# Projections phase of a two-block vision kernel: key and value turns and their sums in one stretch of small tiles, relu of the queries on ScalarE, the next image loaded in four pieces

## The chip, the core and the metric

The kernel runs on one core of one Trainium2 chip. The metric is the device time of one execution in microseconds (us); shorter is better. The engines are TensorE (PE in the rows; PEld is its weight load), VectorE (DVE), ScalarE (ACT), GpSimd (POOL) and SyncE (SP), each with its own queue of instructions, ordered among each other by semaphores only.

## The reference, cut to what matters

For 8 images of 256 channels and 64x64 pixels the reference does a window mixing with a residual, and then, on the group-normed result, a linear attention with a residual:

```python
qkv = einsum('bchw,oc->bohw', gn(x), w_qkv)          # 256 -> 768 channels
y = depthwise 5x5 of qkv, then grouped 1x1            # "convolved heads"
mqkv = concat([qkv, y], axis=1)                       # 64 heads of 3*8 channels
q, k = relu(first 8), relu(second 8);  v = third 8, and a row of ones
vk = einsum('bhdn,bhen->bhde', v, k)                  # sums over the 4096 pixels
out = einsum('bhde,bhen->bhdn', vk, q);  out = out[:8] / (out[8] + eps)
x = x + batchnorm(w_proj @ out)
```

The projections phase, which the change is about, computes `qkv` for the unconvolved heads, stores it (for the convolution) and the relu of q (for the output phase), and forms `vk` of these heads: keys and values are turned, so that pixels lie on the partitions, and multiplied.

## The kernel before

Four phases follow each other: window mixing, projections, convolved heads, output. All is written out by hand; each engine's order is the order of the code, and every wait is a semaphore count.

**Projections.** 8 images, and for each 8 chunks of 512 pixels (`NCH = 8`), 64 chunks in all. Images 0, 1 and the last two are written out; the four between run in a hardware loop over pairs (`over_image_pairs`). For each chunk:

- ScalarE makes the normalised pixels of the chunk ahead (`normal`, two halves, L975), and their high part (`high`, L986); VectorE subtracts for the low part (`split`, L1217).
- TensorE forms six output tiles, `product(b, n, 0..5)` (L1125), each of 6 matmuls of 512 columns, in three PSUM banks: tile j uses bank j % 3, and must wait until the tile that had it is copied out. Order: key 0, value 0, key 1, value 1, query 0, query 1.
- ScalarE copies the keys (`key(u)`, L1045) and query 0; VectorE copies the values (`value(n, u)`, L1270) and query 1 (L1305).
- TensorE turns tile pair u (`turn`, L1139: 8 transposes of 128x128) after products 2 and 4, ScalarE takes them out of PSUM (`turned(u)`, L1050 with relu for the keys and L1053), and after product 5 TensorE adds this chunk's share to the sums (`sum_vk`, L1151: 16 matmuls of 32 columns of weights for each pair).
- VectorE and GpSimd write differences and borders of every tile into `stage` (`keys_values`, `queries`; DVE L1223 to L1229, POOL L902 to L937), which SyncE's queue stores to `qkv_scratch`; GpSimd makes the relu of the queries (L941), and SyncE stores it to `qr_scratch`. `stage` has two buffers, used in turn by even and odd chunks: a buffer is written again when its stores have landed.
- In chunks 1 to 4 VectorE also takes the statistics of the next image (`moments`, `norm_moments`, one quarter a chunk), after the copy of query 1; at the end of chunk 4 it gathers them, in chunk 5 `centre` and in chunk 5 `variance` follow, with two small matmuls of TensorE between (`means`, `variances`), in chunk 6 `scale`.
- At the end of an image ScalarE issues the load of the image after the next, 4 MB in one transfer (L1087); its statistics are taken from chunk 1 of the next image on.

Of the kernel before, what the change touches and what calls it, by code (L numbers as in the profile page):

```python
# [25 lines left out]
ALU = mybir.AluOpType  # L26
ACT = mybir.ActivationFunctionType
# [153 lines left out]
def make_constants(nc, ctx, two_phases, K):  # L181
# [7 lines left out]
    K["vk"] = sb("vk_table", [P, KT, B, D + 1])  # L189
# [14 lines left out]
    K["p_mv"] = sb("pmv", [P, CT, 2])  # L204
    K["p_norm"] = norm_tiles(sb, lambda name: ctx.enter_context(nc.semaphore(name)), "p")
# [45 lines left out]
def window_mixing(nc, K, x_in, w_mix, b_mix, w_qkv, w_dw, x1_dram, taps_dram):  # L251
# [3 lines left out]
    with ExitStack() as ctx:  # L255
# [30 lines left out]
        def norm_of(b):  # L286

            return (0, K["p_norm"][0], K["p_mv"], K["p_norm"][1], None) if b == B else (b, T, mv, ns, mean)
# [448 lines left out]
def projections(nc, K, x1_dram, qkv_dram, qr_dram, w_pw, bn_in, taps_dram, sorted_dram):  # L737
# [3 lines left out]
    with ExitStack() as ctx:  # L741
# [25 lines left out]
        vT = sb("vT", [P, 2, 4, NSQ, VS])  # L767
# [8 lines left out]
        t_ps = psum("pt_ps", [P, 2, 512])  # L776
        vk_ps = psum("vk_ps", [P, 2, 512])
        stat_bank = psum("pstat_ps", [P, 512])
        stat_ps = stat_bank[:, 0:4]
        pw_ready, pw_turned = K["pw_ready"], sem("pw_turned")  # L780
        std_in, std_out, bn_link = sem("bn_var"), sem("bn_std"), sem("bn_chain")
        qs_ready_late = sem("qs_ready_late")

        w_loaded, w_turned, w_split = K["wq_loaded"], sem("wq_turned"), sem("wq_split")
        zeroed, bordered = sem("zeroed"), sem("bordered")
        x_loaded = [sem(f"x1_loaded{i}") for i in range(2)]
# [8 lines left out]
        vk_full, vk_taken = sem("vk_full"), sem("vk_taken")  # L795
# [23 lines left out]
        def _(sp):  # L819
# [17 lines left out]
            def body(i, last):  # L837
                for par in range(2):
# [14 lines left out]
                    def queries(n):  # L853
# [4 lines left out]
                        if last and par == 1 and n == NCH - 1:  # L858
                            sp.wait_ge(qs_ready_late, 1)
                        else:  # L860
                            own.wait_ge(qs_ready, NCH * b + n + 1)
# [4 lines left out]
                    for n in range(NCH):  # L866
                        keys_values(n, 0)
                        if n > 0:
                            queries(n - 1)
                        keys_values(n, 1)  # L870
# [9 lines left out]
        def cells_free(eng, g):  # L880

            at_least(eng, t_full, 4 * (g - 1))
            at_least(eng, kv_diff, 2 * (g - 1))
            at_least(eng, kv_odd, 2 * (g - 1))
# [7 lines left out]
        def _(pool):  # L892
            pool.memset(vT[:, :, :, :, SQ:VS], 1.0).then_inc(zeroed, 1)

            def body(i, last_body):
                for par in range(2):
# [7 lines left out]
                    def border(n):  # L904
# [5 lines left out]
                        pool.memset(stage[:, n % 2, :, :, :, row, :].rearrange("p t a k x -> p (t a) k x"), 0.0)\  # L910
                            .then_inc(bordered, 1)
# [17 lines left out]
                    def queries(n, end=False):  # L929
# [4 lines left out]
                        at_least(pool, K["qr_stored"][n % 2], 32 * (4 * b + n // 2))  # L934
# [3 lines left out]
                        if end:  # L938
                            return
                        for t in range(2):  # L940
                            last = pool.tensor_scalar(qs[:, n % 2, t, :], qw[:, n % 2, t, :], 0.0, None, ALU.max)  # L941
                        last.then_inc(qs_ready, 1)

                    for n in range(NCH):
                        if n % 4 < 2:
                            border(n)
                        keys_values(n, 0)
                        if n > 0:
                            queries(n - 1)
                        keys_values(n, 1)  # L950
                    queries(NCH - 1, last_body and par == 1)
# [3 lines left out]
        def _(act):  # L955
# [58 lines left out]

            def pointwise(step):
# [5 lines left out]
                elif step == 1:  # L1021
                    act.wait_ge(pw_turned, 1)
                    act.activation(K["pw"][:, 0:4 * HT, :].rearrange("p g o -> p (g o)"), stat_bank[:, :], ACT.Copy)\
                        .then_inc(pw_ready, 1)
                elif step == 2:
# [3 lines left out]
                    act.activation(K["pw"][:, 4 * HT:6 * HT, :].rearrange("p g o -> p (g o)"), stat_bank[:, 0:2 * P], ACT.Copy)\  # L1029
                        .then_inc(pw_ready, 1)  # L1030

            def body(i, last_body):
                for par in range(2):
                    b = 2 * i + par
                    for n in range(NCH):
# [4 lines left out]

                        def key(u):
# [5 lines left out]
                        def turned(u):  # L1047
                            act.wait_ge(t_full, 4 * g + 2 * u + 1)
                            at_least(act, vk_full, g)
                            act.activation(kT[:, u, :, :].rearrange("p a c -> p (a c)"), t_ps[:, 0, :], ACT.Relu)\  # L1050
# [1173 lines left out]
```

## Time and profile before

| | us |
|---|---|
| median of 3 runs | 2488.25 |
| lowest, highest | 2484.59, 2489.66 |
| profiled execution: time, span | 2490.49, 2488.8 |
| busy in the span: TensorE, VectorE, ScalarE, GpSimd | 2364.8, 1992.4, 1495.8, 1099.0 |

The profiled execution is one further run; its span is the time from the first to the last instruction. Busy shares are means over four phases with different limits, so the projections are read by themselves. In the rows a start is in us from the span's start, and the projections lie from about 261 to 1015 us. Matmuls overlap, so the busy time of TensorE says little: what counts is the distance from one start to the next.

### The profile page before, as it was taken

How to read it: one execution, taken by the hardware profiler on the slowest of the kernel's cores; microseconds unless marked ns; L12 is line 12 of the kernel's file. 1: busy time of each engine (PE TensorE's matmuls, PEld its weight loads, DVE VectorE, ACT ScalarE, POOL GpSimd, SP SyncE). 2: the span in 40 equal slices, each digit the busy share in tenths (PEclk: the TensorE clock that was granted, in tenths of full speed). 3: DMA queues.
4: the chain of work that ended last, by engine and by line, in shares of the span. 5: the costliest groups of instructions: out<-in, count | busy, mean ns of one | idle time of the engine just before them, and what ended most of it. 6: DMA issues, size and time to landing. Idle time of an engine off the chain costs nothing. (4 is left out here: it accounts for less than half of the span.)

```text
span 2488.8 us, 66780 instructions
## 1 busy us (share of the span) xinstructions
PE 2364.8 (95%) x25485; PEld 1886.2 (76%) x25485; DVE 1992.4 (80%) x2652; ACT 1495.8 (60%) x1864; POOL 1099.0 (44%) x1477
## 2 busy tenths in 40 slices
PE   5999799999999999799999999999999889999998
PEld 5889687777787788577888888888888656666666
DVE  7887588787688786788888888888888578888775
ACT  5777576665566566566677677667767433443342
POOL 6722387787787787300000000000000068888887
PEclk9999899999999999899999999999999999999999
DMA  7874688988889889988888888888888677777774
GB/s 283 342 293 177 212 301 313 325 294 306 307 281 323 320 282 321 267 204 204 206 213 208 208 208 210 207 207 212 210 206 209 215 251 271 279 278 271 270 271 135
DMA packets 300877, 628.38 MB, mean 252 GB/s; under 512 B 50688, under 2 KB 252160, under 8 KB 291456
## 3 DMA queue, kind: packets, MB, share of 16 engines
q1 hardware_dynamic: 295616, 590.90, 77.1%
q10 hardware_dynamic: 4048, 31.11, 3.5%
q0 software_dynamic: 1008, 3.67, 0.4%
q8 instruction: 125, 2.05, 0.3%
q14 instruction: 80, 0.66, 0.1%
HBM read 327.81 MB, written 300.94 MB: 253 GB/s over the span
## 5 line engine op out<-in xcount | busy, mean ns | idle before, releaser
L1901 POOL TENSOR_TENSOR ql<-image,qh 128x1024 fp32r<-128x1024 f32 x128 | 305.3, 2410 | 971.4 <-ACT qh L1929 971.4
L1555 PE MATMUL c_ps<-dh,wh 128*128 128x512 f32 x1152 | 463.5, 402 | 17.5 <-DVE wl L1706 13.1
L1470 ACT ACTIVATE dh<-image 128x1632 fp32r<-128x1632 f32 x192 | 301.5, 1570 | 266.7 <-PE c_ps L1555 250.6
L1555 PE MATMUL c_ps<-dh,wl 128*128 128x512 f32 x1152 | 455.0, 395 | 0.0
L1555 PE MATMUL c_ps<-dl,wh 128*128 128x512 f32 x1152 | 453.6, 394 | 1.3 <-issue 1.3
L1664 DVE TENSOR_TENSOR dl<-image,dh 128x1632 fp32r<-128x1632 f32 x192 | 356.4, 1856 | 72.2 <-ACT dh L1470 72.2
L1125 PE MATMUL o_ps<-xh,wqh 128*128 128x512 f32 x768 | 320.8, 418 | 11.0 <-issue 7.6
L1125 PE MATMUL o_ps<-xl,wqh 128*128 128x512 f32 x768 | 304.6, 397 | 0.0
L1125 PE MATMUL o_ps<-xh,wql 128*128 128x512 f32 x768 | 303.4, 395 | 0.0
L1555 PEld LDWEIGHTS c_ps<-dh,wh 128*128 128x128 f32 x1152 | 217.7, 189 | 70.1 <-DVE wl L1706 13.2
L1555 PEld LDWEIGHTS c_ps<-dl,wh 128*128 128x128 f32 x1152 | 217.3, 189 | 53.4 <-issue 1.3
L1555 PEld LDWEIGHTS c_ps<-dh,wl 128*128 128x128 f32 x1152 | 217.5, 189 | 45.8
L941 POOL TENSOR_SCALAR qs<-qw 128x512 f32<-128x512 f32 x126 | 234.2, 1874 | 0.0
L1045 ACT ACTIVATE kv<-o_ps 128x512 f32<-128x512 f32 x128 | 76.9, 601 | 260.2 <-PE o_ps L1125 256.7
L2037 PE MATMUL z_ps<-qh,fh 128*128 128x512 f32 x512 | 208.5, 407 | 5.2 <-ACT qh L1929 3.6
L1950 ACT ACTIVATE zs<-z_ps,bn_shift 128x512 f32<-128x512 f32 x64 | 44.0, 687 | 281.6 <-PE z_ps L2037 281.6
L2037 PE MATMUL z_ps<-qh,fl 128*128 128x512 f32 x512 | 200.7, 392 | 0.0
L2037 PE MATMUL z_ps<-ql,fh 128*128 128x512 f32 x512 | 200.5, 392 | 0.0
L1270 DVE COPY kv<-o_ps 128x512 f32<-128x512 f32 x128 | 87.9, 687 | 123.8 <-PE o_ps L1125 123.1
L975 ACT ACTIVATE xn<-image,p_nb,p_sc 128x512 f32<-128x512 f32 (+2 forms) x160 | 175.8, 1121 | 8.4 <-PEq L255 8.4
L902 POOL TENSOR_TENSOR ptick<-ident 128x1 f32<-128x1 f32 x224 | 95.4, 426 | 184.7 <-DMA qkv_scratch<-stage 78.5
L1125 PEld LDWEIGHTS o_ps<-xh,wqh 128*128 128x128 f32 x768 | 146.4, 191 | 39.7 <-issue 14.1
(210 smaller groups left out, 5024.0 us busy)
## 6 DMA issues: line engine op xcount, KB each, us to landing
qkv_scratch<-stage SPq DMA_DIRECT2D x384, 408.0 KB, 4.0
image<-qkv_scratch SPq DMA_DIRECT2D x189, 816.0 KB, 6.3
qr_scratch<-qs SPq DMA_DIRECT2D x128, 256.0 KB, 3.0
yq_scratch<-qy SPq DMA_DIRECT2D x64, 512.0 KB, 6.7
image<-qr_scratch SPq DMA_DIRECT2D x128, 256.0 KB, 6.2
image<-yq_scratch SPq DMA_DIRECT2D x128, 256.0 KB, 5.9
ox<-x_scratch SPq DMA_DIRECT2D x8, 4096.0 KB, 14.8
out<-ox SPq DMA_DIRECT2D x7, 4096.0 KB, 12.7
```

Source lines behind the costliest of these rows:

```text
L902: pool.tensor_tensor(tick[:, k:k + 1], K["ident"][:, 0:1], K["ident"][:, 1:2], ALU.add)
L941: last = pool.tensor_scalar(qs[:, n % 2, t, :], qw[:, n % 2, t, :], 0.0, None, ALU.max)
L975: last = act.activation(dst[:, :, to:to + rows, :], src[:, :, of:of + rows, :], ACT.Identity, bias=T["nb"][:, ct:ct + 1], scale=T["sc"][:, ...
L1045: act.activation(kv[:, n % 2, 2 * u, :], o_ps[:, (2 * u) % 3, :], ACT.Copy).then_inc(kv_ready, 1)
L1125: last = pe.matmul(o_ps[:, j % 3, :], w[:, ct, P * t:P * t + P], xx[:, n % 2, ct, :], start=(k == 0), stop=(k == 5))
L1270: dve.tensor_copy(kv[:, n % 2, 2 * u + 1, :], o_ps[:, (2 * u + 1) % 3, :]).then_inc(kv_ready_v, 1)
L1470: act.activation(dh[kind][:, :], raw[kind], ACT.Copy).then_inc(hi_ready, 1)
L1555: last = pe.matmul(c_ps[:, m, :], w[hp][:, kind, part, o:o + P], cells[:, :, HALF * dy:HALF * dy + HALF * NB], start=(k == 0), stop=(k == 5))
L1664: dve.tensor_tensor(dl[kind][:, :], raw[kind], dh[kind][:, :].bitcast(F32), ALU.subtract)\
L1901: pool.tensor_tensor(two_of(ql, n, tp), two(n, tp), two_of(qh, n, tp).bitcast(F32), ALU.subtract)\
L1950: act.activation(zs[:, :], z_ps[:, 1, :], ACT.Identity, bias=bn["shift"][:, 1:2]).then_inc(z_taken, 1)
L2037: last = pe.matmul(z_ps[:, o, :], w[par][:, t, P * o:P * o + P], d, start=(m == 0), stop=(m == 3 * KT - 1))
```

## The change

In the projections:

- `turn` is now done once a chunk, for both pairs, as 64 transposes of 32 rows x 128 columns each (the form that the phase of the convolved heads already uses, L1565). Four row groups write four PSUM banks. `sum_vk` of the chunk before stands directly ahead of it, for both pairs, and both stand between product 4 and product 5. ScalarE takes out the keys and the values with one instruction of 1024 elements each. The sums of an image are taken (`take_sums`) in chunk 1 of the next.
- TensorE waits, ahead of this stretch, for both keys and both values of the chunk (`kv_ready`, `kv_ready_v` at 2 * g + 2).
- The relu of the queries moves from GpSimd to ScalarE (`positive`), one chunk later.
- The image is loaded in four pieces of 1 MB (`load_quarter`), at the heads of chunks 0 to 3 of the next image, and VectorE waits for each quarter by itself.
- VectorE's order in a chunk changes: `split` goes ahead of the second value, and `queries(n - 1)` to the end. ScalarE's: both normals and `high` stand ahead of the second key. GpSimd and SyncE take both pairs ahead of the queries.
- `means` stands in chunk 5 and `variances` and `variance` in chunk 6, and the mean is copied to SBUF.

In the convolved heads one semaphore takes the place of two; in the output phase the table `vk` has an index moved by 2.

```diff
+            def load_quarter(b, par, quarter):
+                if quarter == 0:
+                    act.wait_ge(x_free, b)
+                    for g in range(GROUPS):
+                        act.wait_ge(K["x_stored"][par][g], 16 * PIECES[g] * (B // 2))
+                rows, part = slice(P * (quarter // 2), P * (quarter // 2) + P), slice(H * W // 2 * (quarter % 2), H * W // 2 * (quarter % 2 + 1))
+                act.dma_start(x1[par][:, quarter // 2, part], x1_dram[b - 1, rows, part]).then_inc(x_loaded[quarter], 16)
...
+                        if n < 4 and (par == 1 if isinstance(b, int) and b < 2 else True) and not (last_body and par == 1):
+                            load_quarter(b, 1 - par, n)
+                        if more:
+                            normal(*ahead, 0)
                         key(0)
                         if more:
-                            normal(*ahead, 0)
+                            high(ahead[0], ahead[1], normal(*ahead, 1))
...
                         key(1)
-                        turned(0)
-                        if more:
-                            high(ahead[0], ahead[1], normal(*ahead, 1))
...
+                        if not isinstance(g, int) or g > 0:
+                            positive(b, n - 1)
                         act.wait_ge(o_full, o0 + 5)
                         queries_read(act, g)
                         act.activation(qw[:, n % 2, 0, :], o_ps[:, 1, :], ACT.Copy).then_inc(q_ready, 1)
-                        turned(1)
+                        turned()
...
-            def turn(b, n, u):
+            def turn(n):
                 for s in range(2):
-                    for a in range(4):
-                        last = pe.transpose(t_ps[:, s, P * a:P * a + P], kv[:, n % 2, 2 * u + s, P * a:P * a + P],
-                                            K["ident"][:, :])
-                    last.then_inc(t_full, 1)
+                    for u in range(2):
+                        for a in range(4):
+                            at = SQ * (8 * s + 4 * u + a)
+                            for q in range(NSQ):
+                                rows = slice(SQ * q, SQ * q + SQ)
+                                last = pe.transpose(t_ps[:, q, at:at + SQ], kv[rows, n % 2, 2 * u + s, P * a:P * a + P],
+                                                    K["ident"][rows, rows])
+                last.then_inc(t_full, 1)
...
                         product(b, n, 2)
-                        turn(b, n, 0)
                         product(b, n, 3)
                         product(b, n, 4)
-                        turn(b, n, 1)
+                        pe.wait_ge(kv_ready, 2 * g + 2)
+                        pe.wait_ge(kv_ready_v, 2 * g + 2)
+                        if n > 0:
+                            sum_vk(b, n - 1)
+                        elif not isinstance(b, int) or b > 0:
+                            sum_vk(b - 1, NCH - 1)
+                        turn(n)
                         product(b, n, 5)
-                        for u in range(2):
-                            sum_vk(b, n, u)
```

TensorE, in a chunk of the first image, in the program before: the second `turn` of a chunk, product 5, the sums, and the head of the next chunk (`pt_ps` are the turned tiles, `o_ps` the products, `vk_ps` the sums).

```order
L1139 MATMUL pt_ps<-ident,kv 128x128 x8
L1125 MATMUL o_ps<-xh,wqh 128x512
L1125 MATMUL o_ps<-xh,wql 128x512
L1125 MATMUL o_ps<-xl,wqh 128x512
L1125 MATMUL o_ps<-xh,wqh 128x512
L1125 MATMUL o_ps<-xh,wql 128x512
L1125 MATMUL o_ps<-xl,wqh 128x512
L1151 MATMUL vk_ps<-vT,kT 32x33 x32
L1125 MATMUL o_ps<-xh,wqh 128x512
```

The same place after the change, from the end of product 4 to the head of product 5.

```order
L1130 MATMUL o_ps<-xh,wql 128x512
L1130 MATMUL o_ps<-xl,wqh 128x512
L1161 MATMUL vk_ps<-vT,kT 32x33 x32
L1143 MATMUL pt_ps<-ident,kv 128x32 x64
L1130 MATMUL o_ps<-xh,wqh 128x512
L1130 MATMUL o_ps<-xh,wql 128x512
```

The sums have moved from behind product 5 to ahead of the turns, and there is one stretch a chunk where there were three.

VectorE, in chunk 2 of the first image, before: value 0, its differences (`stage<-kv`), the query differences of the chunk before (`stage<-qw`), value 1, its differences, `split`, query 1, and a quarter of the statistics.

```order
L1270 COPY kv<-o_ps 128x512 [waits kv_diff,kv_odd,pt_full,o_full]
L1228 TENSOR_TENSOR stage<-kv 128x4x128 [waits qkv_stored0,kv_ready_v,kv_ready]
L1229 TENSOR_TENSOR stage<-kv 128x4x16x7
L1223 TENSOR_TENSOR stage<-qw 128x4x16x7 [waits q_ready_v,q_ready]
L1225 TENSOR_TENSOR stage<-qw 128x4x128
L1270 COPY kv<-o_ps 128x512 [waits o_full]
L1228 TENSOR_TENSOR stage<-kv 128x4x128 [waits qkv_stored0,kv_ready_v,kv_ready]
L1229 TENSOR_TENSOR stage<-kv 128x4x16x7
L1217 TENSOR_TENSOR xl<-xn,xh 128x1024 [waits xh_ready]
L1305 COPY qw<-o_ps 128x512 [waits q_odd,qs_ready,q_diff,o_full]
L111 BN_STATS pbst<-image 128x6 x4
```

The same chunk after the change.

```order
L1300 COPY kv<-o_ps 128x512 [waits kv_diff,kv_odd,pt_full,o_full]
L1247 TENSOR_TENSOR stage<-kv 128x4x128 [waits qkv_stored0,kv_ready_v,kv_ready]
L1248 TENSOR_TENSOR stage<-kv 128x4x16x7
L1236 TENSOR_TENSOR xl<-xn,xh 128x1024 [waits xh_ready]
L1300 COPY kv<-o_ps 128x512 [waits o_full]
L1247 TENSOR_TENSOR stage<-kv 128x4x128 [waits qkv_stored0,kv_ready_v,kv_ready]
L1248 TENSOR_TENSOR stage<-kv 128x4x16x7
L1242 TENSOR_TENSOR stage<-qw 128x4x16x7 [waits q_ready_v,q_ready]
L1244 TENSOR_TENSOR stage<-qw 128x4x128
L1341 COPY qw<-o_ps 128x512 [waits q_odd,qs_ready,q_diff,o_full]
L111 BN_STATS pbst<-image 128x6 x4
```

`split` (`xl<-xn,xh`) now stands ahead of the second value's copy, where the query differences stood, and these stand last.

## Rows read from the trace of the kernel before

**Rows 1.** Busy us by engine, granted clock, DMA share and GB/s, in two stretches

```profile
core 0: us, PE busy (x) PEld busy (x) DVE busy (x) ACT busy (x) POOL busy (x), PEclk, DMA share, GB/s
468.00:479.00 11.00, 9.38 (x75) 7.63 (x62) 5.14 (x9) 6.55 (x9) 2.09 (x6) 1.00 1.00 361
586.00:597.00 11.00, 10.85 (x129) 8.90 (x119) 10.21 (x16) 7.08 (x10) 8.90 (x12) 1.00 0.83 296
```

**Rows 2.** One line's instructions: L1125, ns min/median/max, first and last start

```profile
L1125 PE MATMUL o_ps<-xh,wqh x768: 387/391/776, 267.2 to 1012.9; 128*128 128x512 f32 x192
```

**Rows 3.** Timeline of TensorE, one chunk in the loop: start us, us

```profile
682.28 0.76 PE L1151 MATMUL vk_ps<-vT,kT 128*32 128x33 f32 x64
683.20 0.47 PE L1125 MATMUL o_ps<-xh,wqh 128*128 128x512 f32 x1
...
687.15 0.39 PE L1125 MATMUL o_ps<-xl,wqh 128*128 128x512 f32 x1
687.39 1.03 PE L1139 MATMUL pt_ps<-ident,kv 128*128 128x128 f32 x8
688.18 0.48 PE L1125 MATMUL o_ps<-xh,wqh 128*128 128x512 f32 x1
...
694.28 0.47 PE L1125 MATMUL o_ps<-xh,wqh 128*128 128x512 f32 x1
```

**Rows 4.** Timeline of TensorE: heads of chunks 5 and 6, and of two outside the loop

```profile
705.39 0.47 PE L1125 MATMUL o_ps<-xh,wqh 128*128 128x512 f32 x1
...
717.40 0.47 PE L1125 MATMUL o_ps<-xh,wqh 128*128 128x512 f32 x1
...
913.38 0.47 PE L1125 MATMUL o_ps<-xh,wqh 128*128 128x512 f32 x1
...
924.29 0.47 PE L1125 MATMUL o_ps<-xh,wqh 128*128 128x512 f32 x1
```

**Rows 5.** Timeline of TensorE in the convolved heads: last product, sums, next product

```profile
1299.97 0.40 PE L1555 MATMUL c_ps<-dl,wh 128*128 128x512 f32 x1
1300.30 0.77 PE L1583 MATMUL yvk_ps<-yvT,ykT 128*32 128x33 f32 x64
...
1302.11 0.50 PE L1555 MATMUL c_ps<-dh,wh 128*128 128x512 f32 x1
```

**Rows 6.** Timeline of ScalarE in the convolved heads: the turned tiles taken out

```profile
1302.37 1.03 ACT L1493 ACTIVATE yvT<-yt_ps 128x1024 f32<-128x1024 f32 x1 [0.39 <-PE yt_ps L1565]
1303.29 1.02 ACT L1486 ACTIVATE ykT<-yt_ps 128x1024 f32<-128x1024 f32 x1
```

**Rows 7.** Timeline of VectorE, ends of chunks 4 and 7, head of chunk 6

```profile
458.26 0.21 DVE L1321 TENSOR_TENSOR pdiag<-vk_ps,sqmask 128x64 f32<-128x64 f32 x1
...
458.51 0.29 DVE L1325 TENSOR_REDUCE vk_table<-pdiag 128x16 f32<-128x64 f32 x1
...
705.40 2.46 DVE L111 BATCH_NORM_STATS2 pbst<-image 128x6 f32<-128x512 f32 x4
...
708.62 0.69 DVE L1270 COPY kv<-o_ps 128x512 f32<-128x512 f32 x1
...
720.64 0.69 DVE L1270 COPY kv<-o_ps 128x512 f32<-128x512 f32 x1 [3.27 <-PE o_ps L1125]
721.53 0.69 DVE L1228 TENSOR_TENSOR stage<-kv 128x512 f32<-128x512 f32 x1 [0.20 <-DVE kv L1270]
...
722.69 0.75 DVE L1223 TENSOR_TENSOR stage<-qw 128x448 f32<-128x448 f32 x1
```

**Rows 8.** One line's instructions: VectorE's split, ScalarE's normal, high, image load

```profile
L1217 DVE TENSOR_TENSOR xl<-xn,xh x64: 1206/1214/1666, 265.7 to 1000.1; 128x1024 fp32r<-128x1024 f32 x64
...
L975 ACT ACTIVATE xn<-image,p_nb,p_sc x160: 426/1284/1353, 261.1 to 996.8; 128x512 f32<-128x512 f32 x96, 128x480 f32<-128x480 f32 x32, 128x32 f32<-128x32 f32 x32
...
L986 ACT ACTIVATE xh<-xn x64: 1042/1062/1072, 264.6 to 998.2; 128x1024 fp32r<-128x1024 f32 x64
...
L1087 ACTq DMA_DIRECT2D image<-x_scratch x6: 384/394/404, 363.9 to 831.6; - x6
```

**Rows 9.** Timeline of VectorE, chunk 2 of the first image

```profile
300.39 0.69 DVE L1228 TENSOR_TENSOR stage<-kv 128x512 f32<-128x512 f32 x1 [6.16 <-DMA qkv_scratch<-stage]
```

More of the change, by code:

```diff
@@ L857, in queries @@
                         tile(n, 4, q_stored)
[L858 to L861, printed above, removed]
+                        own.wait_ge(qs_ready, NCH * b + n + 1)
                         for t in (1, 0):
@@ L1146, in sum_vk @@
+            def sum_vk(b, n):
+                pe.wait_ge(k_turned, NCH * b + n + 1)
+                pe.wait_ge(v_turned, NCH * b + n + 1)
                 if n == 0:
                     at_least(pe, vk_taken, 2 * b)
-                for a in range(4):
+                if n == 0:
                     for q in range(NSQ):
                         ch = slice(SQ * q, SQ * q + SQ)
-                        last = pe.matmul(vk_ps[ch, u, 0:VS], kT[:, u, a, ch], vT[:, u, a, q, :],
-                                         start=(n == 0 and a == 0), stop=(n == NCH - 1 and a == 3))
@@ L1153, in sum_vk @@
-                if u == 1:
-                    last.then_inc(vk_full, 1)
+                        pe.matmul(vk_bank[ch, 0:SUMMED], zeros[:, 0:SQ], zeros[:, :], start=True, stop=False)
+                for u in range(2):
+                    for a in range(4):
+                        for q in range(NSQ):
+                            ch = slice(SQ * q, SQ * q + SQ)
+                            last = pe.matmul(vk_ps[ch, u, :], kT[:, u, a, ch], vT[:, q, u, a, :],
+                                             start=False, stop=(n == NCH - 1 and a == 3 and u == 1))
@@ L1262, in body @@
                     npar, ni = (1, i) if par == 0 else (0, i + 1)
-                    gather, centre, variance, scale = norm_scale(dve, Chain(dve, ns["chain"]), b + 1, T, mv, bst, stat_ps, ns)
+                    gather, centre, variance, scale = norm_scale(dve, Chain(dve, ns["chain"]), b + 1, T, mv, bst, stat_ps, ns,
+                                                                K["p_mean"])
                     def value(n, u):
@@ L1288, in body @@
                         value(n, 0)
-                        keys_values(n, 0)
                         if nxt and n == 5:
                             centre()
-                        if n > 0:
-                            queries(n - 1)
-                        value(n, 1)
-                        keys_values(n, 1)
+                        if nxt and n == 6:
+                            variance()
+                        keys_values(n, 0)
+                        if n == 1 and (not isinstance(b, int) or b > 0):
+                            take_sums(b - 1)
                         if n < NCH - 1:
@@ L1302, in body @@
                             dve.tensor_copy(T["t1"][:, 0:1], K["ident"][:, 0:1]).then_inc(x_free, 1)
+                        value(n, 1)
+                        keys_values(n, 1)
+                        if nxt and n == 6:
+                            scale()
+                        if n > 0:
+                            queries(n - 1)
                         dve.wait_ge(o_full, QT * g + 6)
@@ L1483, in take_k @@
             def take_k(s):
[L1484 removed]
+                act.wait_ge(turned, s + 1)
                 at_least(act, vk_full, 2 * s)
@@ L1558, in convolve, with turn @@
                     last.then_inc(m_full, 1)
-            def turn(src, out, full):
+            def turn(src, out):
                 for a in range(8):
@@ L1565, in turn @@
                         last = pe.transpose(out[:, r, SQ * a:SQ * a + SQ], src[rows, P * a:P * a + P], K["ident"][rows, rows])
-                last.then_inc(full, 1)
+                return last
             def turn_ready(s):
@@ L1608, in _ @@
                 sum_vk(s - 1, pair)
-            turn(vy, vt_ps, vt_full)
-            turn(ky, kt_ps, kt_full)
+            turn(vy, vt_ps)
+            turn(ky, kt_ps).then_inc(turned, 1)
             for pair in range(2):
```

169 lines of the change are left out of this document (81 added, 88 removed).

## The prediction

> **What bounds the kernel now.** I read three views of the projections: the starts of TensorE's matmuls, the timeline of VectorE and ScalarE beside them, and the share of the DMA engines. The phase goes from 267 to about 1013 us, some 746 us for 64 chunks [rows 2]. In an undisturbed chunk TensorE never stops: 17 steps from 683.20 to 687.15 take 3.95, that is 0.08 for a slow first step and 0.228 a matmul, so the 36 matmuls cost 8.2 us; a turn costs from 687.38 to 688.18, 0.8 us, twice; the rest of the 11.11 us from one head to the next (694.28 to 705.39) is the sums and the resumption [rows 3, 4]. Outside the loop a chunk takes 10.91 us (913.38 to 924.29), chunk 5 of an image 12.01 (705.39 to 717.40), 0.90 more, since `means` waits for the gathered statistics [rows 4]. Added up: 32 x 11.11 + 32 x 10.91 + 7 x 0.9 = 711 us. The other 35 us are stalls. Their picture is the first row of group 1: while the 4 MB load is under way the DMA engines are full (share 1.00, 361 GB/s) and VectorE works 5.14 of 11 us, GpSimd 2.09; an ordinary chunk needs a share of 0.83 [rows 1]. The stage buffers come free late, then the copies out of PSUM, then TensorE. One such wait of 6.16 us stands in the first image, where no load has been issued yet but SyncE's queue sorts the taps [rows 9]. I count about 8 of the 35 us to the first image and 27 to the six loads.
>
> So the bound is TensorE's issue in every chunk, and the DMA engines once an image.
>
> **TensorE's stretch.** What the change puts there exists already: in the convolved heads the same 32 sum products (64 records) and 64 small transposes stand between two large products. From the start of the last large matmul (1299.97) to that of the next (1302.11) is 2.14 us, less its own 0.23 leaves 1.91 [rows 5]. TensorE alone would then need 8.2 + 0.08 + 1.91 = 10.2 us a chunk, 0.9 less than in the loop and 0.7 less outside. It has one resumption where it had three. The sequencer's waits ahead of product 0 now stand behind six long matmuls and should be hidden.
>
> A rule speaks against it: by the Trainium skill, "TensorEngine Tiling (Array Packing)", section Key Properties, changing the tiling mode drains the engine, and the new stretch has two small modes (32 columns, then 32 rows) and so three changes a chunk, where the old chunk had one small mode and two. The trace agrees that a change is not free: the sums start 0.33 us behind the last large matmul and not 0.23 [rows 5]. One more drain of that 0.1 would be 6 us over 64 chunks by the rule taken by itself; by the row, which has all three changes in it, nothing is to be added to the 1.91. I take the row.
>
> **What is late next: VectorE.** TensorE now asks for value 1 of the chunk before it may sum and turn, and ahead of its copy VectorE has value 0, its differences and `split`. Counted from a head C: value 0 started 3.24 us behind the head (720.64 less 717.40), 3.16 without the slow first step; the differences 0.89 later, the instruction behind them 1.16 later, at 5.21 [rows 4, 7]; `split` 1.21, its median [rows 8]; the copy 0.69 [rows 7]. The value is ready at C + 7.1, and with 0.1 for the restart at 7.2. TensorE is through with product 4 at 30 x 0.228 = 6.84, and would start at 6.94. It waits 0.26 us: **10.5 us for an ordinary chunk**. Behind the waiting matmul stand product 5 and through it query 1, the statistics and the next value 0.
>
> The ends differ with VectorE's load. If its value is in time for other reasons the chunk is 10.2. `split` has also taken 1.67 [rows 8], when GpSimd was working beside it; its long instruction was the relu, which leaves it, so I take the medians.
>
> ScalarE must deliver xh for that `split`: it takes the turned tiles from 0.26 behind product 5's start (1302.37 less 1302.11) [rows 5, 6], which is C - 1.2, in two steps of 0.92 [rows 6], then two normals of 1.28 and `high` 1.06 [rows 8] and one copy like VectorE's 0.69 [rows 7]. That ends at C + 4.95, in time for 5.21. With 0.39 for issuing a piece of the load [rows 8] it is 5.34, so chunks 0 to 3 may lose 0.1. The relu of the queries (1024 elements, like `high` 1.06) comes behind key 1, in time that ScalarE has: it is busy 7.08 of 11 us [rows 1]. Moving it costs nothing as long as that gap is there; without the gap it would cost up to 1.06 a chunk. GpSimd loses its longest work, busy 8.90 of 11 [rows 1], and nobody waits for that.
>
> Chunk by chunk of an image:
> - chunk 0: 10.6; chunk 1: plus 0.54 for taking the sums (458.26 to the end at 458.80) [rows 7], now in VectorE's chain: 11.0;
> - chunks 2 to 4 follow a chunk with statistics: query 1 starts 0.42 behind product 5's end (as 720.64 does behind product 1's), takes 0.6, the statistics 2.46 [rows 7]: value 0 starts at C + 3.5 and not 3.16: 10.8 each;
> - chunk 5: statistics and gather took 3.22 from 705.40 to 708.62 [rows 7]. They used to start under the sums; now they start at C + 1.0 and end at 4.24, where product 2 could have started at 2.74. With 0.24 for the small matmul TensorE waits 1.75, not about 0.6. Then `centre`, with a copy more, stands ahead of the differences, 0.9 as an estimate from the three small instructions' 0.54 [rows 7]: value 1 is ready at 4.24 + 2.05 + 0.9 + 1.21 + 0.69 + 0.1 = 9.2, against 6.94 + 1.75: 0.5 more. 12.45 in all;
> - chunks 6 and 7: 10.5; `variance` fits in the 0.2 that the differences wait for their own value.
>
> An image takes 10.6 + 11.0 + 32.4 + 12.45 + 21.0 = 87.5 us, seven 612; the last, without statistics, 8 x 10.5 + 0.5 and 2 for the pointwise turns, 86.5. Together 699 where 711 stood: **the merged stretch brings 12 us**, of the 52 that TensorE's own count promises.
>
> **The load in pieces.** An ordinary chunk keeps the DMA engines busy 0.83 x 11 = 9.1 us [rows 1]; 4 MB at 361 GB/s are 11.6 us, 2.9 a piece. Chunks 0 to 3 then want 12.0 us of DMA in 10.7, so the stores fall behind by 1.3 a chunk, 5 us at the end, and catch up in chunks 4 to 7. Before, 11.6 us came at once. A stage buffer has the whole chunk between its stores and its next use: stores of chunk n are issued by C + 10 and wanted at C + 21 + 4 for VectorE, some 8 us more than the 4 or 5 that they need. A backlog of 5 fits in that, one of 11.6 did not. So I let 24 of the 27 us go and leave 3. The price of this step lies between 0 and 27.
>
> **The sum**, against the profiled execution (2490.49, with a span of 2488.8): 12 + 24 = 36 us less, 2454.5. The median of the runs shown is 2.2 us lower, so **2452 us**. The phases before and behind don't change: the last image's relu and sums end within a microsecond of where they did.
>
> **The rivals.**
> - *The DMA engines stay the bound.* Chunks 0 to 3 run at 12.0 and not 10.8: 5 us more in six images, so 30 of the gain go, and with the loads' 3 about 6 to 15 us are left: 2475 (2470 to 2482). For it: 8 x 9.1 + 11.6 = 84.4 of 87.5 us, a share of 0.97. Against it: 9.1 is from a chunk that still worked off stores. By the Trainium skill, "DMA: Bandwidth & Descriptors", section Queues, rings and completion order, each DMA engine takes whole packets from its queues in turn, so a piece still delays the stores beside it; nothing here shows how long. Chance 0.20.
> - *VectorE isn't late.* Chunks of 10.2, then the DMA engines bound an image at 84.4: 7 x 84.4 + 82.5 = 673, 26 us better: 2426. Against it: the chain above has medians only. Chance 0.07.
> - *Slower: VectorE's chain is late by much.* One mechanism: GpSimd, held up by a stage buffer, works beside VectorE during differences and `split`, which then take 1.67 as the longest one did [rows 8] and half as much more for the differences: value 1 is ready at 7.1 + 0.46 + 0.6 = 8.2, a wait of 1.3 a chunk. 64 x 1.05 = 67 us more than forecast: 2519 at worst. It decides from 36 / 64 = 0.56 us a chunk on. Chance 0.08.
> - *Nothing comes of it*: stretch and wait cancel (0.2 more wait a chunk), and the load's stall returns in the chunks with pieces: 2485 to 2492. Chance 0.07.
>
> **How the numbers follow.** Forecast 0.58, own range 2442 to 2465. With the first rival's 2482 as the upper end nearly reached and the second's 2426 left out, the range is 2438 to 2478. A difference under 0.2% (5 us) is about what a measurement of this kernel can't tell from no change: faster 0.85 (forecast and the first two), same 0.07, slower 0.08.
>
> **What would show it.** Right: one stretch a chunk, with 1.8 to 1.9 us from its first sum product to product 5; heads 10.4 to 10.6 us apart in quiet chunks, with the sums' wait put down to VectorE's value copy or to issue; chunk 5 at 12.2 to 12.7 us; no stall over 2 us in chunks 0 and 1 from the second image on; VectorE without the long waits for stores. Wrong: a stretch over 2.2 us; heads 10.2 apart (VectorE in time) or over 11 (late); a DMA share of 1.0 through chunks 0 to 3 with VectorE waiting for stores; TensorE at 1.2 GHz behind chunk 5's wait.

## The result, and the profile after

| | before | after |
|---|---|---|
| median, us | 2489.66 (2484.59 to 2491.81, 9 runs) | 2500.18 (2493.84 to 2509.44, 9 runs) |
| profiled execution, us (span) | 2490.49 (2488.8) | 2493.84 (2491.9) |
| projections, first to last product's start | 267.2 to 1013.3 | 267.9 to 1013.3 |
| records of TensorE's products, whole span | 25485 | 28621 |

The ratio is 1.0042, with an interval of 1.0029 to 1.0056: **slower, where 2452 us was forecast, and outside the range**. The projections alone were to get shorter, by 36 us. They got shorter by 1. The traced execution of after is the fastest of its nine: it lies 3 us above before's, the medians 10.5 us apart. The readings below account for the 3; where the other 7 go no trace shows.

First the quiet chunks. The timeline of TensorE, two chunks in the loop (start us, us), which answers to [rows 3, 5]:

```profile
706.52 0.77 PE L1161 MATMUL vk_ps<-vT,kT 128*32 128x33 f32 x64
707.21 1.20 PE L1143 MATMUL pt_ps<-ident,kv 32*128 32x32 f32 x64
708.35 0.50 PE L1130 MATMUL o_ps<-xh,wqh 128*128 128x512 f32 x1
...
716.98 0.77 PE L1161 MATMUL vk_ps<-vT,kT 128*32 128x33 f32 x64
717.67 1.19 PE L1143 MATMUL pt_ps<-ident,kv 32*128 32x32 f32 x64
718.79 0.50 PE L1130 MATMUL o_ps<-xh,wqh 128*128 128x512 f32 x1
```

From one product 5 to the next are 10.44 us, where the forecast said 10.5 and the old chunk took 11.11. The stretch takes 1.83 us from its first sum to product 5. The same stretch in a chunk where VectorE is just late:

```profile
461.67 0.39 PE L1130 MATMUL o_ps<-xl,wqh 128*128 128x512 f32 x1
462.51 0.76 PE L1161 MATMUL vk_ps<-vT,kT 128*32 128x33 f32 x64 [0.45 <-DVE kv L1300]
463.20 1.19 PE L1143 MATMUL pt_ps<-ident,kv 32*128 32x32 f32 x64
464.32 0.50 PE L1130 MATMUL o_ps<-xh,wqh 128*128 128x512 f32 x1
```

Start to start the sums come 0.84 behind the last large product, 0.51 more than the 0.33 of [rows 5]; the releaser is the forecast one, the copy of value 1. So far the kernel does what was forecast: of the 63 distances from head to head 31 are at most 10.75 us.

Now the others. TensorE's weight loads, from product 4 of another chunk on (idle time ahead of a group in brackets), and VectorE beside them:

```profile
568.93 0.19 PEld L1130 LDWEIGHTS o_ps<-xl,wqh 128*128 128x128 f32 x1
570.66 0.67 PEld L1161 LDWEIGHTS vk_ps<-vT,kT 128*32 128x32 f32 x64 [1.55 <-issue]
571.38 0.94 PEld L1143 LDWEIGHTS pt_ps<-ident,kv 32*128 32x128 f32 x53
575.20 0.40 PEld L1143 LDWEIGHTS pt_ps<-ident,kv 32*128 32x128 f32 x11 [2.89 <-issue]
575.67 0.29 PEld L1130 LDWEIGHTS o_ps<-xh,wqh 128*128 128x128 f32 x1
```

```profile
569.92 0.68 DVE L1300 COPY kv<-o_ps 128x512 f32<-128x512 f32 x1
570.68 0.73 DVE L1247 TENSOR_TENSOR stage<-kv 128x512 f32<-128x512 f32 x1
```

The 1.55 us ahead of the sums end when the copy of value 1 does (569.92 + 0.68 = 570.60), called issue or not. The 2.89 us are something else. They stand between the 53rd and the 54th transpose of one group, where the program has no wait, 1.6 us after the last tile that the group reads was ready. In the projections I count nine such stops of 1.6 to 3.9 us from one start to the next, 25 us in all: six inside the turns, three inside a product that follows soon after a stretch. In the list of waits of this phase (us in total, times, longest) the six inside the turns are most of the second row, which does not tell what is missing:

```profile
PEld vk_ps L1161 <- issue: 39.4, 55, 7.8
PEld pt_ps L1143 <- issue: 17.9, 7, 3.7
```

What comes just ahead of each end is a packet of the instruction queue. The one of this stop started at 572.85 and took 1.07 us; TensorE went on 1.28 us behind its end. In seven of the nine the packet started only after TensorE had already stopped, and the restart is 1.3 to 1.5 us behind the packet's end in all nine (1.3 to 1.6 in e7, below), 2.2 to 2.6 behind its start. The two kernels' packets in the projections (queue and kind: packets, MB, share of 16 engines), before and after:

```profile
q8 instruction: 62, 1.02, 0.5%
```

```profile
q8 instruction: 85, 1.39, 0.7%
```

A packet is 16 KB. With it go the busy times of the stretch, before and after (columns as in [rows 1], which count TensorE's products and weight loads behind their busy times):

```profile
267.00:1014.00 747.00, 717.42 (x7433) 584.19 (x7436) 575.78 (x873) 463.35 (x687) 568.18 (x759) 0.98 0.86 300
```

```profile
267.00:1014.00 747.00, 690.39 (x10532) 562.71 (x10530) 546.84 (x881) 517.51 (x622) 375.67 (x635) 0.95 0.88 300
```

10532 + 10530 less 7433 + 7436 are 6193 more records for 23 more packets, 269 a packet. So the packets are TensorE's program, some 270 instructions each, and a stretch of 128 records of sums and 128 of turns is about a whole packet, used up in 1.83 us, less than the 2.2 to 2.6 us from a packet's start to TensorE's restart. Six products use 72 records in 8.2.

Full DMA engines are not needed while TensorE stands. The last 2.1 us of the stop at 610.3 (columns as in [rows 1]) have a DMA share of 0.00:

```profile
610.30:612.40 2.10, 0.21 (x13) 0.10 (x6) 0.87 (x2) 0.00 (x0) 2.10 (x5) 1.00 0.00 0
```

Its packet had started at 609.77, when the stores had all but ended; in the half us ahead of six of the other eight packets the engines were full. So whether the stores make the packets start late is open.

The second loss is the clock. Behind a stop and in the chunk after it (columns as above):

```profile
691.00:694.60 3.60, 0.83 (x51) 0.72 (x47) 1.59 (x3) 0.00 (x0) 0.00 (x0) 0.81 0.46 150
695.00:702.00 7.00, 6.88 (x28) 5.09 (x24) 3.81 (x9) 4.53 (x5) 3.56 (x11) 0.64 0.67 219
702.00:710.00 8.00, 8.00 (x155) 6.63 (x156) 6.53 (x13) 5.16 (x7) 2.35 (x7) 1.00 0.61 194
```

TensorE idles for 3 us, and from inside the stop on (0.81 in the first row) the granted clock is 1.2 in place of 2.4 GHz for some 7 us. Over the phase the trace has 67 us at 1.2 GHz, before 27; the mean clocks above are 0.95 and 0.98. This chunk took 14.9 us where the same chunk of most other images takes 10.4: 4.5 more for a stop of 3.0. In the second row of the three GpSimd, the DMA engines and the vector engines are slack too: everybody waits for TensorE.

**The sum closes.** I give each position in an image the middle of its five shortest periods (10.53, 10.89, 10.55, 10.43, 10.34, 11.92, 10.45 and 10.25 us for chunks 0 to 7) and take the 64 together:

| us | before | after |
|---|---|---|
| 64 undisturbed chunks | 714 | 683 |
| stops for instructions | 0 | 25 |
| long wait in the first image's chunk 2 | 6 | 8 |
| loop branch | 4 | 4 |
| later waits for value 1, or for stage buffers through it | 12 | 7 |
| rest: products at 1.2 GHz and small things | 10 | 18 |
| projections | 746 | 745 |

The chunks got shorter by more than the 12 us forecast, namely 31, and the later waits by 5. Of these 36 us 25 went into the stops, 8 into the lower clock (the difference of the two rests, so an estimate), 2 into the first image. That the gains add up to the forecast's 36 is chance: forecast were 12 and 24. The forecast's own sign of being wrong, a stretch over 2.2 us, stands in nine stretches: the six with a stop inside and three that ran at the lower clock. Outside the phase after is slower by a few us more: behind the last product, inside the last sums, stands a tenth stop of 2.65 us, again with a packet ahead of its end; the heads start 1.5 us later (1029.0 against 1027.5), and the spans differ by 3.1.

### The profile page after: what moved, and what is told of

Same layout as the page of the kernel before. It is cut to its first block and busy times, and to the rows that moved or that the text cites. A ratio compares the mean times of both kernels' runs of the same rounds, so it can differ in the third digit from the quotient of the medians.

```text
span 2491.9 us, 72450 instructions
## 1 busy us (share of the span) xinstructions
PE 2337.1 (94%) x28621; PEld 1863.7 (75%) x28621; DVE 1962.2 (79%) x2661; ACT 1550.8 (62%) x1799; POOL 907.2 (36%) x1352
## 5 line engine op out<-in xcount | busy, mean ns | idle before, releaser
L1581 PE MATMUL c_ps<-dh,wh 128*128 128x512 f32 x1152 | 463.9, 403 | 13.3 <-DVE wl L1732 11.3
L1130 PE MATMUL o_ps<-xh,wql 128*128 128x512 f32 x768 | 308.6, 402 | 2.3 <-issue 2.3
L904 POOL TENSOR_TENSOR ptick<-ident 128x1 f32<-128x1 f32 x224 | 121.0, 540 | 379.9 <-DMA qkv_scratch<-stage 216.9
L1130 PEld LDWEIGHTS o_ps<-xl,wqh 128*128 128x128 f32 x768 | 149.6, 195 | 37.9 <-issue 5.1
L1130 PEld LDWEIGHTS o_ps<-xh,wql 128*128 128x128 f32 x768 | 149.8, 195 | 30.5 <-issue 1.4
L2150 DVE TENSOR_TENSOR image<-image,bc_ps 128x1024 f32<-128x1024 f32 x128 | 149.2, 1207 | 6.5 <-PE bc_ps L2049 6.5
## 6 DMA issues: line engine op xcount, KB each, us to landing
ox<-x_scratch SPq DMA_DIRECT2D x8, 4096.0 KB, 14.9
```

The lines of the kernel that those rows point to most:

```text
L904: pool.tensor_tensor(tick[:, k:k + 1], K["ident"][:, 0:1], K["ident"][:, 1:2], ALU.add)
L1130: last = pe.matmul(o_ps[:, j % 3, :], w[:, ct, P * t:P * t + P], xx[:, n % 2, ct, :], start=(k == 0), stop=(k == 5))
L1581: last = pe.matmul(c_ps[:, m, :], w[hp][:, kind, part, o:o + P], cells[:, :, HALF * dy:HALF * dy + HALF * NB], start=(k == 0), stop=(k == 5))
L2150: dve.tensor_tensor(at, at, bc_ps[:, 2 * tp:2 * tp + 2, :], ALU.mult).then_inc(q_scaled, 1)
```

## The experiments

All ratios are to the kernel before, run on the same chip. The "phase" is the time from the first to the last product's start; "packets" are those of the instruction queue from 267 to 1014 us.

| run | median us | ratio (95% interval) | phase | packets | stops, us | us at 1.2 GHz |
|---|---|---|---|---|---|---|
| after | 2500.18 | 1.0042 (1.0029 to 1.0056) | 745.4 | 85 | 9, 25 | 67 |
| e1 | 2486.37 | 0.9987 (0.9977 to 0.9996) | 737.7 | 63 | 0 | 16 |
| e2 | 2480.10 | 0.9955 (0.9941 to 0.9969) | 732.8 | 88 | 1, 1.7 | 31 |
| e3 | 2490.62 | 1.0005 (0.9993 to 1.0017) | 738.2 | 86 | 8, 20 | 51 |
| e4 | 2474.41 | 0.9936 (0.9919 to 0.9952) | 730.1 | 63 | 0 | 17 |
| e5 | 2461.05 | 0.9910 (0.9890 to 0.9931) | 714.1 | 89 | 0 | 20 |
| e6 | 2472.68 | 0.9955 (0.9939 to 0.9970) | 722.2 | 87 | 5, 13 | 40 |
| e7 | 2541.59 | 1.0223 (1.0204 to 1.0242) | 799.8 | 88 | 19, 27 | 23 |
| e8 | 2470.47 | 0.9944 (0.9926 to 0.9963) | 727.1 | 63 | 0 | 16 |
| e9 | 2459.89 | 0.9883 (0.9861 to 0.9904) | 712.5 | 88 | 0 | 26 |
| e10 | 2482.76 | 0.9975 (0.9964 to 0.9986) | 739.9 | 62 | 0 | 12 |

Stops are those over 1.1 us in the phase that end behind such a packet where the program has no wait; that at the loop's branch (2.6 to 5.8 us, in every kernel) is not among them. The last column, too, is of the phase alone; some expectations count from 267 to 1028 us and so have 10 to 20 more. e7's phase ends at 1067; over all of it it has 94 packets.

**e1: the turns as 16 transposes of 128x128, in the same place.**

```diff
-                            at = SQ * (8 * s + 4 * u + a)
-                            for q in range(NSQ):
-                                rows = slice(SQ * q, SQ * q + SQ)
-                                last = pe.transpose(t_ps[:, q, at:at + SQ], kv[rows, n % 2, 2 * u + s, P * a:P * a + P],
-                                                    K["ident"][rows, rows])
+                            last = pe.transpose(t_ps[:, 2 * s + u, P * a:P * a + P], kv[:, n % 2, 2 * u + s, P * a:P * a + P],
+                                                K["ident"][:, :])
```

> The changed kernel with its 64 transposes of 32x128 replaced by 16 of 128x128 in the same place (same sums, same waits, same loads, same two copies out). With 32 instead of 128 turn instructions the stops inside the stretch go, the half-clock time of the projections falls from 78 us to under 45, and although the stretch grows to 2.3 us (+26 us in 64 chunks) the kernel is at 2478 to 2490, faster than the changed one (2500). Theory B, the stops come from the crowding of the DMA engines by the loads and stores: the stops stay, the longer stretch is added, 2515 to 2530.

No stop for a packet is left, and 16 us at 1.2 GHz where after has 67. The price is the turns themselves: 11.0 us a quiet chunk and not 10.5. The kernel is faster than after by 0.55%, though each of its chunks is half a microsecond longer. The 3 us that the expectation gives a fetch are in no row; from a packet's start to the restart are 2.2 to 2.6. Fewer records, no stops: what it does not tell is whether the number or the place counts.

**e2: the sums apart from the turns, between products 1 and 2.** A product of two columns carries the turns' wait.

```diff
                         product(b, n, 1)
+                        if n > 0:
+                            sum_vk(b, n - 1)
+                        elif not isinstance(b, int) or b > 0:
+                            sum_vk(b - 1, NCH - 1)
                         product(b, n, 2)
...
-                        if n > 0:
-                            sum_vk(b, n - 1)
-                        elif not isinstance(b, int) or b > 0:
-                            sum_vk(b - 1, NCH - 1)
+                        pe.matmul(t_ps[:, 0, 0:2], K["gavg"][:, :], zeros[:, 0:2], start=True, stop=True)
                         turn(n)
```

> The changed kernel with the sums of the chunk before moved from ahead of the turns to between products 1 and 2 (one tiny matmul stands ahead of the turns to carry their wait); the number of instructions is the same plus one. Theory A (instructions run out in one long burst): two bursts of 128, four us apart, leave time for a fetch, most stops go, value 1 is in time as well: 2450 to 2470. Theory B (DMA crowding): the stops stay, only VectorE's 0.26 us a chunk is won: about 2485. A third view, that the number of instructions and not the burst matters: no change against 2500 other than that 0.26.

The expected time was missed, but eight of the nine stops are gone with all the records still there; one of 1.7 us is left, inside the first sums behind the loop's branch. What is new stands in chunk 1 of each image, in e2's timeline of TensorE:

```profile
470.50 0.39 PE L1130 MATMUL o_ps<-xl,wqh 128*128 128x512 f32 x1
473.20 0.45 PE L1156 MATMUL vk_ps<-zeros 128*32 128x66 f32 x8 [2.31 <-DVE vk_table L1283]
```

The sums of the new image clear their bank, and VectorE takes the old ones (`take_sums`) only later in that chunk: 2.7 us from start to start here, 2.7 to 2.9 in each of seven images. My edit had made this wait; e5 takes it away.

**e5: e2, with `take_sums` at the end of chunk 0.**

```diff
-                        if n == 1 and (not isinstance(b, int) or b > 0):
-                            take_sums(b - 1)
...
                         if n > 0:
                             queries(n - 1)
+                        elif not isinstance(b, int) or b > 0:
+                            take_sums(b - 1)
```

> The changed kernel with the sums between products 1 and 2, and the sums of an image taken from their bank by VectorE at the end of chunk 0 instead of in chunk 1. In the run with sums apart every chunk took 10.55 us but chunk 1 (13.1 to 14.6), where the sums wait for the bank that VectorE has not yet read. If that wait is the take, chunk 1 falls to 10.6 and the kernel by 20 us from 2480, to 2458 to 2463. If it is a fetch of instructions, chunk 1 stays and the time is 2478 to 2482. Theory A (instructions run out in a burst of 256): no stops inside the turns, whose burst is 128 here.

As expected. In e5's timeline of TensorE a chunk now reads:

```profile
455.98 0.77 PE L1161 MATMUL vk_ps<-vT,kT 128*32 128x33 f32 x64
456.68 0.50 PE L1130 MATMUL o_ps<-xh,wqh 128*128 128x512 f32 x1
...
460.90 0.28 PE L1207 MATMUL pt_ps<-zeros,gavg 128*128 128x2 f32 x2
461.11 1.20 PE L1143 MATMUL pt_ps<-ident,kv 32*128 32x32 f32 x64
462.24 0.50 PE L1130 MATMUL o_ps<-xh,wqh 128*128 128x512 f32 x1
```

and over the phase:

```profile
267.00:1014.00 747.00, 701.76 (x10762) 577.91 (x10761) 574.85 (x917) 536.29 (x632) 356.75 (x646) 0.97 0.91 310
```

The same short instructions, 4.1 us of large products between the two groups, 89 packets, no stop, 10.55 us a chunk. So it is not how many short instructions a chunk has, but how many of them follow on each other. Against after this is 1.3%, from moving one group, with the take that had to go with it.

**e7: the opposite way, the kernel before with long stretches.** The load in pieces as in e4, each sum made twice, so that 256 records stand in one row (numerator and denominator both double).

```diff
-                for a in range(4):
+                for a in range(8):
...
-                        last = pe.matmul(vk_ps[ch, u, 0:VS], kT[:, u, a, ch], vT[:, u, a, q, :],
+                        last = pe.matmul(vk_ps[ch, u, 0:VS], kT[:, u, a % 4, ch], vT[:, u, a % 4, q, :],
```

> The kernel before with its load in pieces, and every sum product done twice (numerator and denominator both double), so that the burst behind product 5 has 256 short instructions of one old form, and no small transposes at all. By their cost alone it is 0.75 x 64 = 48 us slower than without (2474), 2522. Theory A: stops appear inside the sums, where there were none, as in the changed kernel, 8 or more of about 3 us with half clock behind: 2540 to 2570. If the stops belong to the small transposes: 2518 to 2526 and none.

The phase is 69.7 us longer than e4's. 64 more sum records a chunk cost about what the sums take in e5's stretch, 0.70 us (455.98 to 456.68), 45 in all; the rest, 25, is stops inside the sums. One of them, in e7's timeline of the weight loads:

```profile
781.78 0.96 PEld L1154 LDWEIGHTS vk_ps<-vT,kT 128*32 128x32 f32 x97 [0.36 <-issue]
784.89 0.34 PEld L1154 LDWEIGHTS vk_ps<-vT,kT 128*32 128x32 f32 x31 [2.15 <-issue]
```

The packet before that restart went from 782.36 to 783.42, again 1.5 us ahead of it. This kernel has none of the small turns, and it has one kind of short instruction in its stretch and the old order of the rest: neither the change of tiling mode nor VectorE is needed for the stops. They last 1.1 to 2.3 us, shorter than most of after's and than the 3 us expected, and the clock hardly follows (it falls behind two of the 19; 23 us at 1.2 GHz in all). Some 31 packets more than in e4's phase for 8192 more records are about 260 records each. Unlike in seven of after's nine, each packet had started before TensorE stopped, by 0.3 to 1.3 us.

**e3 and e4: what the pieces are worth.** e3 is after with all four pieces issued at the head of chunk 0; e4 is before with the load in four pieces at the heads of chunks 0 to 3.

```diff
-                        if n < 4 and (par == 1 if isinstance(b, int) and b < 2 else True) and not (last_body and par == 1):
-                            load_quarter(b, 1 - par, n)
+                        if n == 0 and (par == 1 if isinstance(b, int) and b < 2 else True) and not (last_body and par == 1):
+                            for quarter in range(4):
+                                load_quarter(b, 1 - par, quarter)
```

> The changed kernel with all four pieces of the load issued at the head of chunk 0. If the pieces are worth what I said (24 us), it is 15 to 25 us slower than the changed kernel, 2515 to 2525, with waits of VectorE for stores in chunks 0 and 1. If the pieces are what crowds the fetches (theory B), it is no slower or faster, 2490 to 2500. Theory A says nothing but that the stops inside the stretch stay, about ten of them.

> The kernel before with only the load in four pieces at the heads of chunks 0 to 3 (one semaphore fewer, and the last relu counts on another). If the load's stalls were worth 27 us and the pieces remove them: 2463 to 2470. From the trace of before, VectorE's late values in chunk 1 of images 1 to 6 were 12.5 us, with the clock behind them perhaps 20: 2470 to 2478. If pieces do nothing or crowd the stores: 2488 to 2495.

In the old kernel the pieces bring 0.64%, 16 us by the ratio and 16 in the phase, not 24. In the changed one they cost: e3 with the load at once has 1.0005 where after has 1.0042, with intervals that don't meet, so it is 0.37% or 9 us faster, and the 15 to 25 us slower that I expected are refuted. Its traced execution has eight stops, 20 us in all, five us less than after's, and behind the first image six waits for value 1 of 1.4 to 3.5 us from start to start, 13 in all, where after has four, 9 in all. So the load at once brings some waits, and the trace with it had fewer us of stops; whether these are the 9 us or single executions scatter so is open.

**e6: after without the six image loads** (the later images are computed from stale pixels).

> The changed kernel without the six loads of the next image (it leaves out those loads and their waits, so images 2 to 7 are computed from stale pixels); bursts of instructions as in the changed kernel. Theory A in its narrow form (a page of 256 instructions used up in 1.9 us is shorter than any fetch): the stops inside the stretch remain, 8 to 11 of them, 2485 to 2495. Theory B (crowding by the pieces): they vanish with the load, and the kernel is at 2440 to 2455. Both needed (a fetch is slow only beside other traffic): between, 3 to 6 stops, 2460 to 2475.

Five stops of 1.9 to 3.4 us remain in the phase, 13 us, against nine and 25. The load isn't needed for them; with it there are more. That is the third of the expectations, in stops and time: the load adds to them, though the stores, which no run takes away, are still there. (That they all go falls, and that all 8 to 11 stay too; and the 0.9% that this kernel is faster than after holds the load's own waits too.)

**e8: e4 with the relu of the queries on ScalarE.**

> The kernel before with the load in pieces and the relu of the queries on ScalarE, one chunk later. ScalarE has 3.9 of 11 us idle, and VectorE's slow splits and differences beside GpSimd's relu are not waited for in an ordinary chunk: 2470 to 2476, the same as with pieces alone (2474.4). If GpSimd's relief shortens the chain to value 1 or the stores' lateness, up to 8 us less; if the relu delays key 1 or query 0, up to 10 us more.

0.9944 against e4's 0.9936, intervals that cover each other: the move brings and costs nothing that can be measured.

**e9 and e10, on e5.** e9 issues `means` behind product 2 in place of product 1 (counted from 0, as in the code) and `centre` behind the differences; e10 has e1's large turns.

```diff
                         product(b, n, 2)
+                        if n == 5 and more:
+                            means()
```

> The kernel of e5 with the group means of the next image's norm issued after product 3 of chunk 5 instead of after product 2 (counting from 1), and VectorE's centring of them behind the first keys and values instead of ahead of them. In e5 chunk 5 takes 12.1 us where the others take 10.55, seven times, and TensorE waits 1.2 to 1.6 us there for the last moments. Theory: TensorE has the wait hidden behind product 3, chunk 5 falls to 10.7, the projections shorten by 7 times 1.4 = 10 us and the run is near 2451 (2447 to 2456). Rival: the VectorE chain is what sets chunk 5 (centring, split and keys lie on it one behind the other), so the wait only moves to the turns at the end of the chunk: 2458 to 2462.

> The kernel of e5 with the turns as 16 transposes of 128x128 in place of 64 of 32x128, otherwise the same order. It has 48 load-and-product pairs fewer in each chunk and no two groups of short instructions next to each other. Theory A (short instructions only cost when they come in one burst that outruns their supply): in e5 nothing is starved in the turns, so the small turns bring their full price there, and e10 is slower by the difference of the two forms, about 0.5 us in each of 56 chunks (10.55 to 11.05): 2483 to 2490, about no change to the kernel before. Rival B (every short instruction costs, wherever it stands): e5 loses to its fetches as well and e10 is no slower than it: 2455 to 2465.

e9: chunk 5 falls from 12.1 to 11.3 us, between the two expectations, since 0.5 us of the wait comes back ahead of the turns; the median lies in the rival's range. 64 undisturbed chunks are 683.4 us against e5's 689.9, and the ratios differ by as much, 0.27%, though their intervals overlap; in the traced execution a wait for value 1 of 5.8 us where e5 has 3.5 hides part of it. e9 has the lowest ratio: 1.2% faster than before, 1.6% faster than after.

e10: 0.9975, against 0.9910 for e5, and 11.09 us a quiet chunk against 10.55. When nothing is starved the small turns are worth 0.65%, 16 us. That is what the small turns are worth on their own, and in after it was spent, and more, on the stops. Against e4, the old order with the load in pieces (0.9936), the rest of the change brings little: e5 is 0.26% lower, with intervals that overlap, and e10, the new order with the large turns, is 0.39% higher, with intervals that don't. Its chunk 5 takes 12.6 us and e4's 11.8, seven times, which is more than half of the 10 us between their phases.

## Why the prediction was wrong, by its own steps

- **The stretch, "by the row ... nothing is to be added to the 1.91".** This is the step that failed. 1.91 us is right for a stretch whose instructions are there (1.83 from the first sum on). It was read from one stretch of a phase where I didn't look for what feeds it, and taken for all 64. In nine of them, or just behind, TensorE ran out of instructions: 25 us, and about 8 more of clock. The term for the supply of instructions was put at nothing without having been looked at. That the supply is the cause is shown from both sides: the stops go when the stretch is cut in two (all but one in e2, all in e5) or thinned (e1), and come in the old kernel when its sums are made as long (e7).
- **VectorE late by 0.26, 10.5 a chunk**: right in the wait and its releaser, and 10.34 to 10.55 in quiet chunks 0 and 2 to 4. Chunk 7 with 10.25 was in time, and chunks 2 to 4 and 5 were put too high by 0.25 to 0.55. The 12 us that the chunks were to bring became 31: here the forecast was too low.
- **The load in pieces, 24 of 27 us**: mis-sized. In the old kernel they bring 16 (e4), in the changed one they cost 9 (e3). I had given the load every stall beyond the first image's 8. By the table above these stalls are 32 us and not 35, 6 of them in the first image; 12 were waits for value 1 or for stage buffers, 4 the loop's branch, and about 10 the lower clock, most of it not behind a load. e4 takes away nearly all that was the load's, as the mechanism said.
- **The relu at nothing**: right (e8).
- **The rivals.** The DMA engines as the bound: no, e5 runs the phase at a share of 0.91, and e6 without loads is still starved. VectorE's chain late by much: its later waits are 7 us in all. The time of "nothing comes of it" (2485 to 2492) is the nearest, by another mechanism. The one that decided wasn't among them.
- **Against the Trainium skill.** I weighed the drains of "TensorEngine Tiling (Array Packing)", Key Properties; the row's 1.91 held. The section of the Trainium skill that bore on the case is "Runtime: NRT & Kernel Launch", Instruction fetch mechanics: instructions come in blocks of 16 KiB, 256 instructions, fetched while the block before is executed, at a cost that it calls "mostly hidden". The trace agrees on size and number (23 more packets for 6193 more records). It disagrees on hidden where a block is used up in 1.8 us: in 9 of 64 places it was not.

Left open: why the packet starts so late (in seven of nine stops after TensorE had stopped), whether the stores beside it delay it, and why nine of the 64 stretches meet an empty supply and the others don't.

## What to carry to other kernels

Small tiles cost records, not only columns. Before joining stretches of short instructions, divide their records (products and weight loads) by 256 (here 246 to 269 a packet) and look at how long one such block lasts: 256 records in 1.8 us starved in 9 of 64 places, 128 and 128 with 4 us of large products between them in none in e5 and in one in e2. A gap called issue in the middle of a group that has no wait is the sign to look for; the end of an instruction packet 1.3 to 1.6 us ahead of its end goes with it.

When two things are moved next to each other because each resumption costs something, ask what else the work between them did: here it gave the supply time.

## What the runs showed of the chip that I had not expected

- A stop for instructions ends 1.3 to 1.6 us behind the end of a 16 KB packet that itself takes about 1 us (0.9 to 1.3 in after's nine), and lasts 1.1 to 3.9 us (5.4 once in e3), with or without an image load beside it, and once in after with the DMA engines at a share of 0.00 for its last 2.1 us.
- With after's seven stops of 2.6 to 3.9 us the granted clock fell to 1.2 GHz for 3 to 7 us, with those of 1.6 and 2.1 us it did not; of e7's 19 stops of 1.1 to 2.3 us two had it. The chunk with the stop at 691.59 lost 4.5 us to it.
- At the loop's branch TensorE stands for 2.6 to 5.8 us between two weight loads, once a phase in every kernel (4.9 in e5, 2.6 in e10).
